# 16-head scores as products over strips of 32 rows, with high and low parts and constant products behind them

## What is computed

```python
def proj(x, W, bias):
    return (x @ W + bias).reshape(b, -1, H, DH).transpose(0, 2, 1, 3)   # H = 16, DH = 8
qh, kh, vh = (proj(q, Wq, bq), proj(k, Wk, bk), proj(v, Wv, bv))
scores = jnp.einsum('bhqd,bhkd->bhqk', qh, kh) / math.sqrt(DH)
scores = jnp.where(mask, -jnp.inf, scores)          # layer 2 only
attn = jax.nn.softmax(scores, axis=-1)
out = jnp.einsum('bhqk,bhkd->bhqd', attn, vh)
out = out.transpose(0, 2, 1, 3).reshape(b, -1, D)
return out @ Wo + bo
```

## Time and profile before

| | us |
|---|---|
| median of 3 runs | 538.87 |
| lowest, highest | 535.52, 541.07 |
| the profiled execution | 544.24 |
| its span | 542.5 |
| TensorE busy in it | 466.8 |
| VectorE, ScalarE, GpSimd busy | 347.2, 253.1, 138.5 |
| mean granted TensorE clock | 0.924 |

### The profile page before, as it was taken

One profiled execution on the slowest core, in us unless ns is written; L12 is line 12 of the kernel. 1 busy time (PEld: TensorE's weight loads), 2 busy tenths in 40 slices (PEclk: granted clock), 3 DMA queues, 4 the chain that ended last, 5 costly groups with the idle time before them and its releaser, 6 DMA issues.

```text
span 542.5 us, 8022 instructions
## 1 busy us (share of the span) xinstructions
PE 466.8 (86%) x2697; PEld 374.8 (69%) x2697; DVE 347.2 (64%) x777; ACT 253.1 (47%) x470; POOL 138.5 (26%) x208
## 2 busy tenths in 40 slices
PE   8779999999999998999998879998538999967085
PEld 4657988999999997889976559885224697733034
DVE  3647787778777776533368766616676654266984
ACT  3536767677677763424422334421430545105811
POOL 4240024302300002201018356514723543010000
PEclk9979999999999998879999999979858998979579
DMA  5869200000000000000000000000000000000001
GB/s 168 243 159 67 13 1 2 1 0 0 0 0 0 0 1 0 1 2 1 1 0 1 0 2 0 1 2 0 0 2 0 0 1 1 1 1 0 0 0 39
DMA packets 28157, 9.63 MB, mean 18 GB/s; under 512 B 17855, under 2 KB 26849, under 8 KB 28129
## 3 DMA queue, kind: packets, MB, share of 16 engines
q1 hardware_dynamic: 26876, 8.66, 9.9%
q10 hardware_dynamic: 1253, 0.61, 0.4%
HBM read 8.74 MB, written 0.52 MB: 17 GB/s over the span
## 4 chain that ended last, share of the span: by engine, by line
PE 68%; DVE 18%; issue 4%; ACT 4%; POOL 2%; DMA 2%; SPq 1%; POOLq 0%; DVEq 0%; ACTq 0%
PE bank L1078 6%; PE bank L463 6%; PE bank L829 6%; PE bank L1113 5%; PE bank L970 5%; PE bank L465 5%; PE bank L464 5%; PE bank L819 4%; PE bank L818 4%; PE bank L458 3%; PE bank L1092 3%; PE bank L850 3%; PE bank L1242 2%; DMA shared<-in_L_xattn_Wo 2%; PE bank L928 2%
## 5 line engine op out<-in xcount | busy, mean ns | idle before, releaser
L1635 DVE TENSOR_TENSOR probT_lo<-bank,probT_hi 128x512 fp32r<-128x512 f32 (+1 forms) x80 | 55.1, 689 | 23.6 <-ACT probT_hi L1327 23.0
L1327 ACT ACTIVATE probT_hi<-bank 128x512 fp32r<-128x512 f32 (+1 forms) x80 | 47.5, 594 | 42.1 <-PE bank L829 41.9
L458 PE MATMUL bank<-ones 128*128 128x512 f32 x110 | 62.6, 710 | 1.8 <-POOL ident L533 1.8
L1628 DVE TENSOR_REDUCE neg_max<-bank 128x1 f32<-128x589 f32 x64 | 49.2, 768 | 19.2 <-PE bank L819 17.8
L1318 ACT ACTIVATE shared<-bank,neg_max 128x589 f32<-128x589 f32 x64 | 48.0, 749 | 6.3 <-DVE neg_max L1628 6.2
L829 PE MATMUL bank<-ident,shared 128*128 128x128 f32 (+1 forms) x320 | 48.0, 272 | 0.4 <-ACT shared L1318 0.4
L602 POOL TENSOR_TENSOR rstd<-var_eps,minus_half 128x4 f32<-128x4 f32 x14 | 14.8, 1056 | 130.0 <-DVE var_eps L1569 130.0
L678 POOL TENSOR_TENSOR scratch<-scratch,neg_max 128x1232 f32<-128x1232 f32 x16 | 36.0, 2248 | 39.2 <-DVE neg_max L1909 39.2
L829 PEld LDWEIGHTS bank<-ident,shared 128*128 128x128 f32 (+1 forms) x320 | 39.8, 142 | 2.7 <-ACT shared L1318 0.6
L1078 PE MATMUL bank<-k_blocks,queries 128*128 128x308 f32 x128 | 36.4, 427 | 5.9 <-DVE scratch L1883 2.2
L458 PEld LDWEIGHTS bank<-ones 128*128 128x128 f32 x110 | 24.1, 235 | 24.8 <-issue 22.8
(11 more groups left out here) (342 smaller groups left out, 1128.0 us busy)
## 6 DMA issues: line engine op xcount, KB each, us to landing
shared<-in_mask_Bx16xSxS_bk SPq DMA_DIRECT2D x8, 154.0 KB, 8.2
shared<-in_L_xattn_Wkv SPq DMA_DIRECT2D x4, 256.0 KB, 7.2
w<-in_L_ffn_W SPq DMA_DIRECT2D x1, 1024.0 KB
shared<-in_L_xattn_Wq SPq DMA_DIRECT2D x2, 256.0 KB, 6.0
x_residual<-in_x ACTq DMA_DIRECT2D x2, 256.0 KB, 6.3
shared<-in_L_xattn_Wo SPq DMA_DIRECT2D x2, 256.0 KB, 8.4
out_x<-x_residual SPq DMA_DIRECT2D x1, 512.0 KB, 3.2
bo<-in_L_xattn_bo SPq DMA_DIRECT2D x3, 64.0 KB, 3.4
```

The source lines that it names most:

```text
L458: nc.tensor.matmul(bank[:, at, :].rearrange("p (n m) -> p n m", n=4), ones[:], ones[:].unsqueeze(1).to_broadcast([P, 4, P]), start=True, s ...
L1327: nc.scalar.activation(probT[HI][0:n, SLOT[c], :], bank[0:n, PT_BANK[b][c], :], ACT.Copy)\
L1628: nc.vector.tensor_reduce(neg_max[:, b, i:i + 1], scores0(i), AX.X, ALU.max, negate=True)\
L1635: nc.vector.tensor_tensor(probT[LO][0:n, SLOT[c], :], bank[0:n, PT_BANK[b][c], :], probT[HI][0:n, SLOT[c], :].bitcast(F32), ALU.subtract). ...
```

## The change

- The keys are spread over four copies instead of sixteen. Copy j holds in each strip of 32 rows (four heads) the rows of the strip's head j and zeros elsewhere; the mask for it, `quad_of_row`, is the sum of four column groups of `head_of_row` and is made once by two small GpSimd operations. The result is split into a high and a low part, `k_blocks[HI]` and `k_blocks[LO]`: three GpSimd operations of 308 elements per batch in place of one of 1232.
- `scores(t)` makes 12 fp32r products in place of 4 fp32 ones. Strip g of 32 rows of queries and keys goes to bank g; high x high for the four strips, then high x low, then low x high.
- The queries need two parts too. ScalarE writes the high part into `qT[HI]`, with the bias but without the scale, which has moved to the keys; VectorE, ahead of its loop over the tiles, makes the low part from the bank and the high part, for both batches.
- TensorE's order: `queries_of(1)` moves ahead of the first scores; behind `scores(1)` come eight constant products; in the loop one constant product stands between `averages(t - 1)` and `transposes(t)` for t = 1 to 6.

```diff
-        k_blocks = sb("k_blocks", [P, B, HM, NC])
+        k_quad = sb("k_quad", [P, 4, NC])
+        k_blocks = [sb(f"k_blocks_{n}", [P, B, 4, NC], F32R) for n in ("hi", "lo")]
...
+            own.add(nc.gpsimd.tensor_tensor(quad_pair[:], head_of_row[:, 0:8].rearrange("p (g j) -> p g j", g=2),
+                                            head_of_row[:, 8:16].rearrange("p (g j) -> p g j", g=2), ALU.add))
+            own.settle()
+            own.add(nc.gpsimd.tensor_tensor(quad_of_row[:], quad_pair[:, 0, :], quad_pair[:, 1, :], ALU.add))
+            own.settle()
...
-                    nc.gpsimd.tensor_tensor(k_blocks[:, b], k16T[:, n, b, :].unsqueeze(1).to_broadcast([P, HM, NC]),
-                                            head_of_row[:].unsqueeze(2).to_broadcast([P, HM, NC]), ALU.mult)\
+                    own.add(nc.gpsimd.tensor_tensor(k_quad[:], k16T[:, n, b, :].unsqueeze(1).to_broadcast([P, 4, NC]),
+                                                    quad_of_row[:].unsqueeze(2).to_broadcast([P, 4, NC]), ALU.mult))
+                    own.settle()
+                    own.add(nc.gpsimd.tensor_copy(k_blocks[HI][:, b], k_quad[:]))
+                    own.settle()
+                    own.add(nc.gpsimd.tensor_tensor(k_blocks[LO][:, b], k_quad[:], k_blocks[HI][:, b].bitcast(F32),
+                                                    ALU.subtract))
+                    own.settle()
...
                     pe.wait_ge(q16_ok, B * n + b + 1)
-                    q = q16T[:, b, (t % TPB) * P:(t % TPB + 1) * P]
                     if t:
                         pe.wait_ge(s16_taken, m)
-                    for g in range(4):
-                        last = nc.tensor.matmul(bank[:, g, 0:BK * NC], q,
-                                                k_blocks[:, b, BK * g:BK * (g + 1), :].rearrange("p h k -> p (h k)"),
-                                                start=True, stop=True)
+                    for stationary, moving in ((HI, HI), (HI, LO), (LO, HI)):
+                        begin, end = stationary == moving, stationary == LO
+                        for g in range(4):
+                            rows = slice(32 * g, 32 * (g + 1))
+                            last = nc.tensor.matmul(bank[:, g, 0:BK * NC],
+                                                    qT[stationary][rows, b, (t % TPB) * P:(t % TPB + 1) * P],
+                                                    k_blocks[moving][rows, b].rearrange("p h k -> p (h k)"),
+                                                    start=begin, stop=end)
...
                 queries_of(0)
                 keep_warm(4, 1)
-                pe.wait_ge(kv16_spread, 8 * B * (n + 1))
+                queries_of(1)
+                pe.wait_ge(kv16_spread, 7 * B * (n + 1))
                 scores(0)
                 scores(1)
-                queries_of(1)
+                keep_warm(4, 8)
...
                     if t:
                         averages(t - 1)
+                        if t < NT - 1:
+                            keep_warm(4, 1)
                     if t < NT:
                         transposes(t)
...
-                    nc.scalar.activation(q16T[:, b, :], bank[:, 6 + b, :], ACT.Identity, bias=bq16[:, n:n + 1],
-                                         scale=SC16).then_inc(q16_ok, 1)
+                    nc.scalar.activation(qT[HI][:, b, :], bank[:, 6 + b, :], ACT.Identity,
+                                         bias=vec_cols[:, row_q:row_q + 1]).then_inc(q16_hi_ok, 1)
...
+                row_q = vrow[f"L{n + 2}_xattn_bq"][0]
+                for b in range(B):
+                    dve.wait_ge(q16_hi_ok, B * n + b + 1)
+                    nc.vector.scalar_tensor_tensor(out=qT[LO][:, b, :], in0=bank[:, 6 + b, :],
+                                                   scalar=vec_cols[:, row_q:row_q + 1],
+                                                   in1=qT[HI][:, b, :].bitcast(F32), op0=ALU.add, op1=ALU.subtract)\
+                        .then_inc(q16_ok, 1)
                 if n == 0:
                     dve.wait_ge(in_mask, 16 * NT)
```

More of the change, by code:

```diff
@@ L194, in build @@
         bo16 = sb("bo16", [P, 2, D])
-        bq16 = sb("bq16", [P, 2])
+        bk16 = sb("bk16", [P, 2])
         head_of_row = sb("head_of_row", [P, HM])
+        quad_pair = sb("quad_pair", [P, 2, 4])
+        quad_of_row = sb("quad_of_row", [P, 4])
         half_of_row = sb("half_of_row", [P, 2])
@@ L362, in build @@
         q16_in_psum = sem("q16_in_psum")
+        q16_hi_ok = sem("q16_hi_ok")
         q16_ok = sem("q16_ok")
@@ L655, in spread_kv @@
                 for b in range(B):
-                    nc.gpsimd.tensor_tensor(k_blocks[:, b], k16T[:, n, b, :].unsqueeze(1).to_broadcast([P, HM, NC]),
-                                            head_of_row[:].unsqueeze(2).to_broadcast([P, HM, NC]), ALU.mult)\
+                    own.add(nc.gpsimd.tensor_tensor(k_quad[:], k16T[:, n, b, :].unsqueeze(1).to_broadcast([P, 4, NC]),
[6 more added lines that the diff above has]
+                    own.settle()
+                    nc.gpsimd.tensor_copy(va_pair[:, n, b, :, :, DH], half_of_row[:].unsqueeze(1).to_broadcast([P, NPAIR, 2]))\
                         .then_inc(kv16_spread, 1)
-                    half = half_of_row[:].unsqueeze(1)
                     by_pair = v_pair[:, n, b, :].rearrange("p (c h d) -> p c h d", c=NPAIR, h=2)
@@ L663, in spread_kv @@
                                                 half_of_row[:, hd:hd + 1], None, ALU.mult).then_inc(kv16_spread, 1)
-                    nc.gpsimd.tensor_copy(va_pair[:, n, b, :, :, DH], half.to_broadcast([P, NPAIR, 2]))\
-                        .then_inc(kv16_spread, 1)
                     by_head = v_left[:, n, b, :].rearrange("p (h d) -> p h d", h=HM)
@@ L1366, in _ @@
             for n in range(2):
-                row = vrow[f"L{n + 2}_xattn_bq"][0] - FIRST
-                nc.scalar.activation(bq16[:, n:n + 1], bank[:, 1, row:row + 1], ACT.Copy, scale=SC16)\
+                row = vrow[f"L{n + 2}_xattn_bk"][0] - FIRST
+                nc.scalar.activation(bk16[:, n:n + 1], bank[:, 1, row:row + 1], ACT.Copy, scale=SC16)\
                     .then_inc(vcol_ok, 1)
@@ L1420, in keys_values @@
                 act.wait_ge(kv16_in_psum, n + 1)
-                row = vrow[f"L{n + 2}_xattn_bk"][0]
                 nc.scalar.activation(k16T[:, n], bank[:, 0, 0:B * NC].rearrange("p (b k) -> p b k", b=B), ACT.Identity,
-                                     bias=vec_cols[:, row:row + 1]).then_inc(kv16_ok, 1)
+                                     bias=bk16[:, n:n + 1], scale=SC16).then_inc(kv16_ok, 1)
                 nc.scalar.activation(v_pair[:, n], bank[:, 1, 0:B * D].rearrange("p (b d) -> p b d", b=B), ACT.Copy)\
```

## The result

| | before | after |
|---|---|---|
| median, us | 539.97 (4 runs) | 560.13 (4 runs) |
| lowest, highest | 535.52, 546.40 | 555.91, 567.79 |
| the profiled execution, and its span | 544.24, 542.5 | 555.91, 554.2 |
| mean granted clock in it | 0.924 | 0.917 |

The ratio is 1.0376, 95% interval 1.0234 to 1.0517; it is one of means, without the slowest run of each kernel (546.40 and 567.79), over 1.5% above its fastest. The forecast was 541.7 with a range to 549.0; the time lies beyond it.

The account below looks back on a forecast made before the run. TensorE alone bound the 16-head stages' loop; after the change the short loop would. 2 x (1.77 + 1.38) - 2.42 - 0.81 - 0.2 = +2.87 on the median 538.87 gave 541.7 us, range 534 to 549.

Parts of the forecast that it names:

- The loops of dependencies: In the 16-head attentions of layers 2 and 3, five tile periods grow from 26.13 to 27.90 us, +1.77 per stage.
- short loop: Averages of one tile, next tile's transposes, ScalarE's two copies, next averages: 4.72 us per tile, 5.58 with constant product.
- S: TensorE time for one tile's scores after the change, strips side by side: 1.06 us, against 2.08 before.
- Rival (a): Strips run one after another, scores taking 1.31 to 1.96 us per tile; kernel 543.2 to 551.3 us; chance 24%.
- The ramp: Start of each 16-head stage up to averages 0, with eight constant products: +1.38 us per stage.
- The clock in the loop: In the tile loop of both 16-head stages TensorE stays at full clock, 5.58 us per tile.
- rival (c): Clock falls inside the loop: +4.8 us for a tile at 1.2 GHz, one per stage, kernel 551 us; chance 11%.
- The ends: Averages 5 to 6 at each stage's end run at full clock: -2.42 us in layer 2, -0.81 in layer 3.
- GpSimd: Key spreading about 0.5 us shorter, twice per layer, slows a VectorE normalisation in layer 3's preparation less: -0.2 us.

Follow-up runs that it names:

- moved-product run: The changed kernel with each tile's constant product moved from between averages and transposes to behind the transposes, ahead of the next scores: 539.4 us, ratio 0.9987.

## Why the prediction was wrong, by its steps

**The loops of dependencies: right.** The short loop with the constant product in it was put at 5.58 us per tile and is 5.62 at 2.4 GHz. Its two parts show one by one: without the product 4.9, with the product where TensorE waits anyway 4.96. That the edit turns the saving on scores into idle time was the forecast, and it is so.

**Scores: right in kind, the size a little high.** S was forecast at 1.06. The moved-product run shows strips 0.63 and behind them averages whose first piece is 0.59 instead of 0.40, together 0.82: three rounds of 0.14 and about 0.4 for what comes once: the two changes between strips and all rows, with the weight loads ahead of the first round. Nine rounds take 1.48 and the same 0.19 behind them, six more rounds for 0.85, 0.14 each. So weight loads of strips are hidden within the stream where I had added 0.109 to each round, and the rest costs 0.4 where I had 0.32. (Twelve all-row products, with no change of rows, take 1.70, 0.06 above their 1.64.) The Trainium skill, TensorEngine Tiling (Array Packing), Tiling Modes, says that a change of mode drains the array and that tiles load and multiply in parallel; the trace agrees with the second (four strips' loads and products start within 0.03 us of each other), and the 0.4 is what the first would leave, though no run parts it from the first loads. In the changed kernel's loop at full clock none of this was in the critical path. Rival (a) is out. The reason that I gave for it, no two products under 0.109 apart in the trace, was a misreading too: the two passes of a one-column product (L790) start 0.03 apart.

**The ramp: near in sum, by luck.** +1.38 per stage was forecast, +0.43 and +2.14 came. The first is at a full clock and shorter than forecast since each scores step in it is (0.63 to 0.69 for 1.06); the second has the clock at 0.91, eight constant products of 8.55 us for 6.88. The two errors nearly cancel. VectorE's low parts did not show as a loss.

**The clock in the loop: the step that failed.** The forecast took the loop's clock as 1.00 on this reasoning: idle times of 1.6 us between scores in the ramp of before had not lowered it, and (for the end of the stage) in the steady loop narrow products and transposes of 3.3 us had not. Both were read in a kernel that had 2.08 us of scores in every tile around them. I gave the case its mechanism and its price per tile (rival (c), +4.8 us for a tile at 1.2 GHz), but one such tile per stage and 11%. Its price was too high for these tiles, which are only in part at 1.2 GHz (+1.3 to +2.4 each in place of +4.8), and its number of tiles too low; that its +9.6 for the loops lies near the +11.7 is luck. Three of the five tiles of each loop were hit by more than a microsecond (layer 2: 7.30, 7.96 and 6.95 against 5.62), +5.8 per stage over the forecast's own 27.9 (33.7), 11.7 in both. With TensorE's idle time filled by useless strip products, and nothing else changed, the clock in the loops is 1.00; that is shown. That it is the idle time as such to which the clock answers is not. The order in which I argued was the fault: I had written down that TensorE would idle more in every tile and asked only whether single gaps were longer than before, not what five such tiles in a row do. Such a tile idles 0.55 us; forecast were 0.4.

**The ends: the same error, smaller.** -2.42 and -0.81 were forecast from a full clock behind averages 5, -0.70 and +0.90 came, 3.4 us in all, with the clock at 0.89 in both. The constant product behind averages 5 did not hold it there; the one ahead of averages 5 does.

**GpSimd.** The normalisation beside the key spreading takes 2.42 us in the chain where it took 3.08, and the next VectorE operation 1.09 where it took 0.72; net -0.3 against the -0.2 forecast, too small to be told in the time.

Sum over the two stages: forecast +3.1, loops +11.7, ends +3.4, ramps -0.2, which is the 18.0 measured. The medians differ by 20.2; the 2 us left over are within the spread of the runs.

## What to carry to other kernels

When a change takes work off TensorE in a loop that then waits for other engines, price the loop at both clocks before counting the gain: here scores shorter by 1.3 us of TensorE per tile (0.82 for 2.08), with a constant product of 0.86 against the clock, ended as 1.5 us more per tile. If constant products are to hold the clock, put them where TensorE waits anyway and look at which instruction releases the next one; with the same product a tile took 5.62 us when it stood ahead of the transposes and 4.96 when it stood behind them. And look at the clock behind a stage before making the stage faster: one product in the right wait gave the old kernel 1.1%.

## What the runs showed that I had not expected

- Twelve strip products of 308 columns, fp32r, over 32 rows each, take 0.42 us of streaming, the time of three; their weight loads are hidden within the stream. To have the clock back in the loops it was enough to issue them three times (1.49 us per tile).
- TensorE's busy share in the records does not tell the clock. The moved-product loop of layer 2 has TensorE busy for 25.80 of 25.80 us and a clock of 0.93; those with strips three times and no constant product are busy for 23.36 of 24.50 and run at 1.00.
- What is still open: which property of TensorE's work lets the clock fall. The loss in the loops goes when their idle time is filled, but a fall also came 22 us into a loop without any. Nor is it settled for the ramp: neither eight products in a row, nor three, nor three spread kept it at 1.00 through every ramp and first tile.
